# A skewed band scratch with the heads innermost, in a kernel of four attention and mixture layers

## The reference

```python
logits = bond_logits - damage * 10.0
logits = jnp.where(cmask[None, None], logits, -jnp.inf)
weights = jax.nn.softmax(logits, axis=-1)
out = jnp.einsum('bntd,bntde->bnte', weights, val_win)
out = out.transpose(0, 2, 1, 3).reshape(Bx, Tx, Cx)
return out @ w_cproj + b_cproj
```

## Time and profile before

| | |
|---|---|
| median of three runs | 3850.13 us (3846.57 to 3855.36) |
| the profiled execution | 3852.74 us; its span, first to last instruction, 3851.0 us |
| granted TensorE clock, mean | 0.878 of full |
| TensorE busy | 3115.1 us, 81% |
| VectorE busy | 2426.6 us, 63% |
| ScalarE busy | 1662.7 us, 43% |
| GpSimd busy | 596.6 us, 15% |
| DMA | 355.91 MB in 331910 packets; 98529 of them under 512 B |
| share of TensorE in the chain that ended last | 52%; of VectorE 28%, of DMA 7% |

### The profile page before, as it was taken

One profiled execution on the slowest core, in us unless ns is written; L12 is line 12 of the kernel. 1 busy time (PEld: TensorE's weight loads), 2 busy tenths in 40 slices (PEclk: granted clock), 3 DMA queues, 4 the chain that ended last, 5 costly groups with the idle time before them and its releaser, 6 DMA issues.

```text
span 3851.0 us, 43741 instructions
## 1 busy us (share of the span) xinstructions
PE 3115.1 (81%) x16174; PEld 1567.3 (41%) x16174; DVE 2426.6 (63%) x4576; ACT 1662.7 (43%) x2458; POOL 596.6 (15%) x425
## 2 busy tenths in 40 slices
PE   3647868997699868997699968998699977996698
PEld 1124423553245433554245532554235532464145
DVE  4634876568756776568765776668755786634442
ACT  3504625465255634465154644446154643432231
POOL 2001000311023010321013010321013110211030
PEclk8568969998799979998699989998799988997696
DMA  3151175302842165402843047412753128412261
GB/s 112 27 95 58 46 123 139 113 14 77 145 144 68 28 106 154 124 22 60 152 133 88 20 104 121 151 39 50 136 133 102 32 81 136 137 58 65 57 203 45
DMA packets 331910, 355.91 MB, mean 92 GB/s; under 512 B 98529, under 2 KB 264225, under 8 KB 330081
## 3 DMA queue, kind: packets, MB, share of 16 engines
q1 hardware_dynamic: 331697, 353.11, 39.1%
HBM read 302.74 MB, written 49.66 MB: 92 GB/s over the span
## 4 chain that ended last, share of the span: by engine, by line
PE 52%; DVE 28%; DMA 7%; ACT 5%; issue 4%; POOL 2%; SPq 2%; ACTq 0%; DVEq 0%; POOLq 0%
DVE MX L1596 7%; PE PS L1805 6%; PE PS L1828 6%; PE PS L1832 5%; PE PS L1659 5%; PE PS L1667 5%; PE PS L1103 3%; DVE U L891 3%; PE PS L1773 3%; DVE U L898 3%; DMA UU<-k_scratch 3%; PE PS L1784 2%; DVE D L1650 2%; POOL D L1404 1%; DVE D L948 1%
## 5 line engine op out<-in xcount | busy, mean ns | idle before, releaser
L1404 POOL TENSOR_TENSOR D<-D,GW 128x512 f32<-128x512 f32 x320 | 434.7, 1359 | 1409.1 <-ACT D L1477 1173.6
L783 ACT ACTIVATE U<-U 128x2048 f32<-128x2048 f32 x256 | 488.0, 1909 | 184.3 <-DVE U L891 99.4
L1645 DVE SCALAR_TENSOR_TENSOR D<-D,PS 128x512 f32<-128x512 f32 x336 | 229.2, 682 | 399.2 <-ACT D L1481 283.6
L1477 ACT ACTIVATE D<-PS 128x512 f32<-128x512 f32 x336 | 200.2, 596 | 610.2 <-PE PS L1828 610.2
L1805 PEld LDWEIGHTS PS<-WST,D 128*128 128x128 f32 (+1 forms) x2688 | 353.0, 198 | 163.4 <-DVE D L1650 96.0
L1805 PE MATMUL PS<-WST,D 128*128 128x128 f32 (+1 forms) x2688 | 380.3, 286 | 29.3 <-DVE D L1650 29.2
L1832 PE MATMUL PS<-XT,WST 128*128 128x512 f32 (+1 forms) x672 | 372.6, 637 | 29.2 <-DVE D L1645 28.0
L898 DVE SCALAR_TENSOR_TENSOR U<-PP,RD,QB 128x512 f32<-128x512 f32 x512 | 364.1, 780 | 47.5 <-ACT QB L780 28.8
L1103 PE MATMUL PS<-U,resident 128*32 128x512 f32 x2048 | 304.6, 675 | 102.3 <-ACT U L783 102.3
L1828 PE MATMUL PS<-XT,WST 128*128 128x512 f32 (+1 forms) x672 | 369.6, 633 | 7.7 <-DMA WST<-in_pairs_dram 4.7
L1596 DVE TENSOR_REDUCE MX<-PS 128x2 f32<-128x1024 f32 x256 | 298.4, 1221 | 84.9 <-PE PS L1751 84.9
(11 more groups left out here) (345 smaller groups left out, 3907.2 us busy)
## 6 DMA issues: line engine op xcount, KB each, us to landing
GW<-gates_scratch SPq DMA_DIRECT2D x320, 256.0 KB, 4.3
WST<-in_pairs_dram SPq DMA_DIRECT2D x336, 192.0 KB, 2.4
U<-band_scratch SPq DMA_DIRECT2D x32, 1280.0 KB, 14.6
UU<-in_w_dram SPq DMA_DIRECT2D x64, 512.0 KB, 7.6
UU<-pad_scratch SPq DMA_DIRECT2D x8, 1792.0 KB
UU<-q_scratch SPq DMA_DIRECT2D x24, 384.0 KB
UU<-k_scratch SPq DMA_DIRECT2D x24, 384.0 KB
e_scratch<-D SPq DMA_DIRECT2D x8, 1024.0 KB, 4.5
```

Source lines behind the costliest of these rows:

```text
L783: e.activation(ring(i), ring(i), ACT.Gelu).then_inc(S["act"], 1)
L1404: e.tensor_tensor(AV[:, n % 3, :], AV[:, n % 3, :], GW[:, p // 2 % GWS, p % 2, :], ALU.mult).then_inc(S["gated"], 1)
```

## The change

The band scratch changes its layout from tile, head, row, column to tile, row, column, head. With that WBT and `band(j)` get the heads innermost, the copy of L799 writes in the order offset, head, the store of a tile has 128 runs of 32 x 16 elements (2 KB), the load 128 runs of 160 x 16 elements (10 KB), and so does the zeroing in the prologue. The moving operand of L1154 is then read at a stride of 16 elements (64 bytes). The number of instructions on every engine stays.

TURN goes from 428.30 to 421.20, and STARTS is replaced by new numbers. Put beside each other, the two tables order the instructions of a full turn alike but for these places: the four band blocks come behind steps 8, 9, 11 and 18 of S1 (before behind steps 23, 27, 31 and at the end, behind L1762), and L1162 behind step 20 (before behind the last block); the first reciprocal of L948 comes behind the 20th maximum of S1 (before both behind L1606), the second behind L1606; L1168 comes three L1784 into S2 (before some 12); SyncE's L714 pad loads come before L1355 (before behind L1358); steps of layer 1 that follow in S2 and behind it come some steps earlier.

```diff
-TURN = 428.30
+TURN = 421.20
 STARTS = {
...
-        z_dram = nc.dram_tensor("band_scratch", (NT, NH, P, BAND), FP32).ap()
+        z_dram = nc.dram_tensor("band_scratch", (NT, P, BAND, NH), FP32).ap()
...
-        band = lambda j: U[:, (j % 3) * NH * BAND:(j % 3 + 1) * NH * BAND].rearrange("p (n t) -> p n t", n=NH)
+        band = lambda j: U[:, (j % 3) * NH * BAND:(j % 3 + 1) * NH * BAND].rearrange("p (t n) -> p t n", n=NH)
...
-        WBT = D[:, 0:4 * T].rearrange("p (j n o) -> p j n o", j=NT, n=NH)
+        WBT = D[:, 0:4 * T].rearrange("p (j o n) -> p j o n", j=NT, n=NH)
...
-                e.dma_start(z_dram[j].rearrange("n p t -> p n t"), zeros[:, 0:NH * BAND].rearrange("p (n t) -> p n t", n=NH)).then_inc(S["scratch_zero"], 16)
+                e.dma_start(z_dram[j].rearrange("p t n -> p (t n)"), zeros[:, 0:NH * BAND]).then_inc(S["scratch_zero"], 16)
...
-                dst = bass.AP(z_dram.tensor, j * NH * P * BAND, [[BAND + 1, P], [P * BAND, NH], [1, HOR]])
-                e.dma_start(dst, WBT[:, j, :, :]).then_inc(S[f"z_stored{j}"], 16)
+                dst = bass.AP(z_dram.tensor, j * NH * P * BAND, [[(BAND + 1) * NH, P], [1, HOR * NH]])
+                e.dma_start(dst, WBT[:, j, :, :].rearrange("p o n -> p (o n)")).then_inc(S[f"z_stored{j}"], 16)
...
-                e.dma_start(band(j), z_dram[j].rearrange("n p t -> p n t")).then_inc(S[f"band{j}"], 16)
+                e.dma_start(band(j), z_dram[j]).then_inc(S[f"band{j}"], 16)
...
-                src = PS(j).rearrange("p (h o n) -> p h n o", h=2, o=HOR)
-                e.activation(WBT[:, j, :, :].rearrange("p (h n) o -> p h n o", h=2), src, ACT.Copy).then_inc(S["soft_act"], 1)
+                src = PS(j).rearrange("p (h o n) -> p h o n", h=2, o=HOR)
+                e.activation(WBT[:, j, :, :].rearrange("p o (h n) -> p h o n", h=2), src, ACT.Copy).then_inc(S["soft_act"], 1)
...
-                                            band(j)[:, 8 * h + 2 * q + r, 0:w], start=(j == 0 and r == 0),
+                                            band(j)[:, 0:w, 8 * h + 2 * q + r], start=(j == 0 and r == 0),
```

More of the change, by code:

```diff
@@ L171, in laid_out @@
     return dict(x=w("L0_attn_x"), consts=packed(CONSTS + MASKS), resident=packed(RESIDENT), passing=packed(PASSING), last=packed(LAST), pairs=wst.reshape(PAIRS, P, 3 * P), w1=w1)
-TURN = 428.30
+TURN = 421.20
 STARTS = {
     "a_act": (
[8 rows of a table removed]
[8 rows of a table added]
     ),
     "a_dve": (
[9 rows of a table removed]
[9 rows of a table added]
     ),
     "a_pe": (
[11 rows of a table removed]
[11 rows of a table added]
     ),
     "a_pool": (
-        1.68, 20.45, 281.18,
+        1.68, 20.05, 273.64,
     ),
     "a_sp": (
-        -64.99, 194.30, 199.03, 213.93, 216.90, 219.88, 222.86, 230.96, 236.26, 241.56, 246.86, 263.68, 293.20, 295.65, 297.45, 303.49,
-        307.14, 357.17,
+        -63.22, 192.47, 196.99, 211.93, 212.85, 213.79, 214.73, 215.98, 216.90, 217.84, 228.00, 239.84, 286.01, 288.83, 290.63, 297.73,
+        302.12, 351.97,
     ),
     "b_act": (
[13 rows of a table removed]
[13 rows of a table added]
     ),
     "b_dve": (
[14 rows of a table removed]
[14 rows of a table added]
     ),
     "b_pe": (
[23 rows of a table removed]
[23 rows of a table added]
     ),
     "b_pool": (
[3 rows of a table removed]
[3 rows of a table added]
     ),
     "b_sp": (
[6 rows of a table removed]
[6 rows of a table added]
     ),
```

## The result

Beside the kernel before (four runs, median 3848.73 us, 3846.57 to 3855.36) the changed kernel took a median of 3884.98 us in four runs (3878.34 to 3886.02): 1.0088 of the time before, 95% interval 1.007 to 1.0105. The profiled execution took 3885.22 us, its span 3883.4 (before 3851.0), the mean granted clock 0.871 (0.878). So the span grew by 32.4 us.

| us | before | after | difference |
|---|---|---|---|
| start to the first S1 | 547.7 | 524.5 | -23.2 |
| six turns, each | 440.46 | 448.44 | +8.0, in all +47.9 |
| the next turn's S1 to the last | 390.2 | 395.9 | +5.7 |
| last S1 to the end | 270.2 | 272.4 | +2.2 |
| S1's start to S2's start, mean of seven | 46.8 | 53.6 | +6.8 |

What follows compares the result with a forecast made beforehand. TensorE was taken to set the pace nearly everywhere, VectorE's maxima filling S1. Prologue -2.8, turn 0 -22, seven turns +45 gave +20 us: 3873 against the profiled execution, 3870 as median; range 3810 to 3945.

Steps and rivals of the forecast that it cites:

- Transfers, turn 0: Longer runs: prologue zeroing -2.8 us; in turn 0 the last band block starts at 203.3 instead of 225.4, -22 us.
- The copy at nothing: L799's copy in the new order costs nothing on ScalarE; bound 0 to 0.3 us for each of four.
- The block at 2.5 us at either clock: An L1154 band block with strided reads takes 2.5 us, the last 2.0, at either clock; bounds 1.3 and 10.0.
- no price: Rival, chance 0.20: the stride in L1154 costs nothing; 3844 us, or 3835 if L1162 stalls little and packing is better.
- a shared reader: Rival, chance 0.18: L1154's strided streams share a reader; two at a time 3945 us (0.10), one at a time 4097 (0.08).
- What a block costs the maxima: VectorE stalls in S1: blocks 1.7, 1.4, 1.4 and 0.9 us, L1162 1.5; sum 6.9 us a turn.
- The reciprocal at 3.3: The first reciprocal, moved among S1's maxima on VectorE, adds 3.3 us a turn.
- S2 8.6 us later: Stalls of 6.9 plus reciprocal 3.3 less today's 1.6 us: S2 starts 8.6 us later after S1's start.
- Comes back 2.1: L1168 no longer trails S2 by 8.1 us, so TensorE regains 2.1 us a turn, leaving +6.5.
- Outside S1, S2 and some places of thread a's scores just behind them the order of instructions stays: The rest of the step table only moves numbers; a smaller TURN with the same order changes nothing.
- is over by then: On SyncE the L714 pad load, moved ahead of L1355, waits for block 4, which is already over.
- The rival of thread b's slack: Rival, chance 0.20: thread b's late start has slack and thread a sets the turn; 3803 to 3829 us, middle 3818.

Runs made afterwards that it cites:

- e6: The kernel before, unchanged, run again on a chip of the experiments: 3879.7 us, ratio 1.000.
- e9: The changed kernel, unchanged, run again on a chip of the experiments: 3892.7 us, 1.003 of the kernel before.
- e3: The changed kernel with L1154 reading dense columns of the same tile (layer 0's attention sums wrong): 3865.4 us, 0.9969 of the kernel before.
- e12: The changed kernel with L1154's blocks 0 to 3 reading at strides of 1, 2, 4 and 8 elements (sums wrong): 3865.6 us in a single execution.
- e11: e5 with only the first reciprocal (L948) and what hangs on it up to L1168 back behind S1: 3843.2 us, 0.9896 of the kernel before.
- e5: The changed kernel with entries due 160 to 196 on TensorE, VectorE and ScalarE back in the old order: 3870.0 us, 0.9974 of the kernel before.
- e8: e5 with the last band block, L1162, L805 and the reciprocals back behind S1: 3892.7 us, 1.0042 of the kernel before.
- e1: The changed kernel with TURN and STARTS of the kernel before, so the new layout alone: 3842.0 us, 0.9904 of the kernel before.
- e10: e8 with SyncE's old order, NMT's rows (L1355) ahead of the L714 pad loads: 3843.6 us, 0.9903 of the kernel before.
- e7: e1 with L1154 reading dense columns (layer 0's attention sums wrong): 3832.7 us, 0.9879 of the kernel before.

## Why the prediction was right, and where it was not

The forecast was 3870 us with 3810 to 3945 around it and slower as the likeliest sign; it took 3885. One step failed by more than the miss, and smaller ones took a part of it back: 23 us of lost time that the sum put at nothing, against some 12 us that S1 cost less than forecast. That the total is off by no more than 15 us is partly luck.

- **Transfers, turn 0: right.** The last block starts 25.0 us earlier (predicted 2.8 + 22), 3.1 of them by luck, as said above. The loads are 3.2 us apart, as worked out, but the first lands 6.5 us after its issue, not 5.2, and the bands gain 20.8 us, not 22. Of the prologue's 2.8 us the chain shows 2.1 (zeros and pad landed at 29.25 instead of 31.35), and layer 0's first work, whose x then takes 6.01 instead of 5.01 us to land, starts 1.1 earlier; between e6 and e9 it is 2.3. The first S1 keeps 23.2.
- **The copy at nothing: right.** L799 takes 0.60 us in either kernel.
- **The block at 2.5 us at either clock: right** (2.36 to 2.50 in all turns, the last 1.95 to 2.05), the time that four streams side by side take if each keeps the pace of L1177. The rival "no price" falls with e3 and e12, "a shared reader" with the blocks themselves.
- **What a block costs the maxima: nearly right.** 1.78, 1.70, 1.04 and 1.20 against 1.7, 1.4, 1.4 and 0.9; L1162 0.31 against 1.5. Sum 6.0 against 6.9. The stride's part, 6.9 less 3.1, was 3.8 us a turn; e3 gives 3.7.
- **The reciprocal at 3.3: right.** e11 gives 2.9 between S1 and S2; its median is 26.8 us lower, 3.8 for each of seven turns; L1168 at full clock again (3.62 to 1.95 us) may be the rest.
- **S2 8.6 us later: 6.8 on the mean,** 7.8 in the turn shown. That S2 starts on NMT's wait, 4.1 us in every turn, with TensorE idle and at half clock, was not in the working; L1168 was priced at its old length.
- **"Comes back 2.1": failed as it stands.** It was 1.1 lost. With the order ahead of the next S1 restored (e5 against e6) it is 2.2 us back, the size of the term. But its reason isn't borne out: the term was for L1168 that no longer trails S2, and e11, where it trails by 8.1 us again, loses only 0.5 of the 2.2.
- **"Outside S1, S2 and some places of thread a's scores just behind them the order of instructions stays": failed.** L1111 ahead of L1832 and L1805, and L914 ahead of L1645, and what moved with them, cost 23 us in all (e5), 3.2 for each of seven turns, which the sum put at nothing. The two tables were at hand before the result; the comparison of them left this place out. With the measured terms the sum is -23.2 + 7 x (6.8 - 2.2) + 23 + 2.2 = +34 us; between the medians it is +36. The 2.2 a turn and the 23 come from other chips than the rest, so that this comes out so close proves little.
- **SyncE's L714 "is over by then": right,** and e8 shows what hung on it.
- **The rival of thread b's slack fell.** What S2 loses, the turn loses: 6.8 and 8.0 us. (The middle of its 3803 to 3829 is 3816, not 3818; nothing hangs on it.)

What stays open: e1 was not run beside the first comparison, where the kernel before doesn't wait for its bands in the full turns. There its gain in turn 0 should hold, but strided blocks in the old places would cost the turns some 1.4 to 2.1 us each. As an estimate from these terms its gain there is -23 + 7 x 1.4 to 2.1, so 8 to 13 us and not 38.

On the chips of the experiments e1, e10 and e11 all beat both kernels, by 1.0% against the one before: the layout with the old order is the version to keep. e7 bounds what a read without the price would add, another 9 us; e12 says that two heads innermost would be enough for such a read; its loads would have runs of 1280 bytes, and it was not tried.

## What to carry to other kernels

A faster transfer doesn't need its consumer moved forward: test the layout and the new order apart, since on the chips of the experiments the layout gave 1% and the order took it back. Work put between two engines that feed each other (maxima and their matmuls) cost much of its length there (1.0 to 1.8 of a block's 2.5 us, the reciprocal 2.9 to 3.8 us), while the wait for a small transfer just behind held such work for nothing. When steps are moved by a table, compare the order on every engine over the whole turn, the DMA queue too: two pad loads in front of three small rows were worth 49 us.

## What the runs showed of the hardware

- A block of L1154 (32 float32 matmul instructions of 160 columns, four side by side) takes 2.5 us at a stride of 4 or 16 elements where dense or at a stride of 2 it takes 1.3 to 1.4, at 2.4 GHz; at 1.2 GHz it is 2.48 to 2.36. From 4 over 8 to 16 the time doesn't grow.
- The same program took 3849 us in the first comparison and 3880 on two chips later, with about the same mean clock (0.878; 0.870 to 0.886), and the ratio of two kernels moved from 1.009 to 1.003 with it. The band stores in 128-byte runs took 17.4 and 20.4 us to landing.
- The zeroing of 5.24 MB moves mostly at 420 to 442 GB/s in runs of 10 KB, in runs of 640 bytes at 335.
